# A delta-rule stage's closing LayerNorm and the next one, done per group inside its output loop

## The chip, the cores and the metric

One core of one Trainium2 chip runs the whole program. The metric is the device time in microseconds of one execution. Three runs of the kernel before took 3671.51, 3671.94 and 3673.90 us; the median is 3671.94.

## The reference

Four layers, each a mixer and a feed-forward part behind a LayerNorm, with residuals, on x of 4 x 1024 x 128 (fp32). What matters here is the end of the fourth mixer and the LayerNorm behind it:

```python
        out = SCALE * out / (denominator + EPS)
        layer_out = jnp.transpose(out, (2, 0, 1, 3)).reshape(slen, bsz, N_HEAD * D_HEAD)
        attn_out = jnp.einsum('sbi,oi->sbo', layer_out, W_o)
        x = h + attn_out
        mu = x.mean(-1, keepdims=True)
        var = ((x - mu) ** 2).mean(-1, keepdims=True)
        return (x - mu) / jnp.sqrt(var + LN_EPS) * ln_g + ln_b
...
    x = x + _L3_attn_ref(_layernorm(x, axis=-1), L3_attn_W_qkvb, L3_attn_W_o, L3_attn_ln_g, L3_attn_ln_b)
    x = x + _L3_ffn_ref(_layernorm(x, axis=-1), L3_ffn_gate_w, L3_ffn_experts)
```

Here h is the normalised input of the mixer, and ln_g, ln_b are vectors of 128 channels. The delta rule runs over the 4 batch entries (the reference calls the first axis the sequence), so for each of the 1024 positions and 16 heads the output of entry t is a sum over the values of entries 0 to t, with scalar weights alpha.

## The kernel before

X holds the residual stream and XN the normalised one, each 128 partitions x 32 tiles x 128 channels (tile t * 8 + j is positions 128 j to 128 j + 127 of batch entry t). XT holds the normalised stream transposed, 128 channels x 4096 tokens. `delta_rule` (from L2164) is a row of stages; each `Stage` ends with a barrier of all engines. The stage "alg" computes alpha on VectorE. The stage "out" works in 8 groups j of 4 units t; n = 4 j + t counts the units, and every engine follows its own list, in order, tied to the others by semaphores:

- TensorE: `sums(j, t)` (L2628) transposes the accumulated heads of unit n, 8 times 128x128, when VectorE has them (`acc_ready`). `values(j + 1, t)` (L2620) makes the values of the same t one group ahead, two matmuls of 512 columns. `project(n - 1)` (L2639) multiplies the transposed heads of the unit before with W_o, 8 matmuls of 128 columns into one of two banks `po`. Each fp32 matmul stands as two records in the profile, a transpose as one.
- ScalarE: two copies of the transposes of unit n out of PSUM into `lT` (L2671), then `take` (L2660), two copies of the values one group ahead.
- VectorE: for unit n one product into `acc` (L2694), t products (L2699) and t additions (L2707), all 128x1024, so 1, 3, 5 and 7 instructions for t = 0 to 3. It may write `acc` of unit n when unit n - 2 is transposed. Behind them `finish(n - 2)` (L2685) waits for the projection of unit n - 2 (`out_mm`) and adds it to the normalised input in XN.

Behind the stage "out" three stages follow. `layernorm` (from L131) on XN, without transposes: 32 BATCH_NORM_STATS2 (L151), a few small instructions, a root on ScalarE (L190), a reciprocal (L164), 32 normalisations (L167), all on VectorE but the root. The stage "fin" loads gain and offset to all partitions, and three VectorE instructions over 128x4096 (L2728 to L2730) scale XN, add the offset to X, and add the two. Then `program` (from L2939) calls `layernorm` on X before the last feed-forward part, this time with 32 transposes on TensorE (L185) and 8 copies on ScalarE (L201) into XT. The next stage, "sink" (`sinkhorn_gates`), begins with a small DMA (L2768) and 32 matmuls that read all of XT (L2780).

Of the kernel before, what the change touches and what calls it, by code (L numbers as in the profile page):

```python
# [15 lines left out]
ALU = mybir.AluOpType  # L16
# [3 lines left out]
P = 128  # L20
BATCH, SEQ, C = 4, 1024, 128
T = BATCH * SEQ
NT = T // P
# [107 lines left out]
def layernorm(nc, X, XN, XT, ident, name, affine=None):  # L131


    with Stage(nc, name) as s:
        stats = s.sb("stats", [P, NT, 6])
        mean, var, tmp, rstd = (s.sb(n, [P, NT]) for n in ("mean", "var", "tmp", "rstd"))
        eps = s.sb("eps", [P, 1])
        aff = s.sb("aff", [P, 2])
        aff_in = s.sem("aff_in")
        tp = [s.ps(f"tp{k}") for k in range(2)]  # L140
        stats_done, var_ready, std_ready, rstd_ready, xn_ready, t_ready, t_copied = (s.sem(n) for n in (
            "stats_done", "var_ready", "std_ready", "rstd_ready", "xn_ready", "t_ready", "t_copied"))
        ch = s.sem("vector_chain")
        with nc.Block() as block:

            @block.vector
            def _(dve):
                c = Chain(dve, ch)
                nc.vector.memset(eps[:], LN_EPS).then_inc(stats_done, 1)
                for i in range(NT):  # L150
                    nc.vector.bn_stats(stats[:, i], X[:, i]).then_inc(stats_done, 1)  # L151
                dve.wait_ge(stats_done, NT + 1)

                nc.vector.tensor_tensor(mean[:], stats[:, :, 1], stats[:, :, 4], ALU.add).then_inc(ch, 1)
                nc.vector.tensor_tensor(tmp[:], stats[:, :, 1], stats[:, :, 4], ALU.subtract).then_inc(ch, 1)
                nc.vector.tensor_tensor(var[:], stats[:, :, 2], stats[:, :, 5], ALU.add).then_inc(ch, 1)
                dve.wait_ge(ch, 3)
                c.n = 3
                c.link(nc.vector.tensor_scalar(mean[:], mean[:], 0.5, None, ALU.mult))
                c.link(nc.vector.tensor_tensor(tmp[:], tmp[:], tmp[:], ALU.mult))  # L160
                c.link(nc.vector.tensor_scalar(tmp[:], tmp[:], 0.25, None, ALU.mult))
                nc.vector.scalar_tensor_tensor(var[:], var[:], 1.0 / C, tmp[:], ALU.mult, ALU.add).then_inc(var_ready, 1)
                dve.wait_ge(std_ready, 1)
                nc.vector.reciprocal(rstd[:], tmp[:]).then_inc(rstd_ready, 1)  # L164
                dve.wait_ge(rstd_ready, 1)
                for i in range(NT):
                    nc.vector.tensor_scalar(XN[:, i], X[:, i], mean[:, i:i + 1], rstd[:, i:i + 1],  # L167
                                            ALU.subtract, ALU.mult).then_inc(xn_ready, 1)

                dve.wait_ge(xn_ready, NT)  # L170

            @block.sync
            def _(sp):
                if affine:
                    for k in range(2):
                        sp.dma_start(aff[:, k:k + 1], affine[k].rearrange("(c a) -> c a", a=1)).then_inc(aff_in, 16)

            @block.tensor
            def _(pe):
                for i in range(NT if XT is not None else 0):  # L180
                    g, k = divmod(i, TPG)
                    pe.wait_ge(xn_ready, i + 1)
                    if k == 0 and g >= 2:
                        pe.wait_ge(t_copied, g - 1)
# [3 lines left out]
            def _(act):  # L188
                act.wait_ge(var_ready, 1)
                nc.scalar.activation(tmp[:], var[:], ACT.Sqrt, bias=eps[:]).then_inc(std_ready, 1)  # L190
                if XT is None:
                    return
# [2802 lines left out]
```

## Time and profile before

| | us |
|---|---|
| median of three runs | 3671.94 |
| profiled execution | 3670.11 |
| its span | 3668.4 |
| output loop (3193.6 to 3404.3) | 210.7 |
| three stages behind it (to 3460.8) | 56.5 |
| the rest of the program behind them | 207.6 |

Over the span TensorE's matmuls are busy 73%, VectorE 58%, ScalarE 39%, GpSimd 26%, and TensorE's mean granted clock is 0.845 of full speed. Such shares are means over many stages with other limits; for a change in one stage its own stretch has to be read, in order of time: what each engine does, how long it stood before it, and which engine released it.

### The profile page before, as it was taken

How to read it: one execution, taken by the hardware profiler on the slowest of the kernel's cores; microseconds unless marked ns; L12 is line 12 of the kernel's file. 1: busy time of each engine (PE TensorE's matmuls, PEld its weight loads, DVE VectorE, ACT ScalarE, POOL GpSimd, SP SyncE). 2: the span in 40 equal slices, each digit the busy share in tenths (PEclk: the TensorE clock that was granted, in tenths of full speed). 3: DMA queues.
4: the chain of work that ended last, by engine and by line, in shares of the span. 5: the costliest groups of instructions: out<-in, count | busy, mean ns of one | idle time of the engine just before them, and what ended most of it. 6: DMA issues, size and time to landing. Idle time of an engine off the chain costs nothing. (4 is left out here: it accounts for less than half of the span.)

```text
span 3668.4 us, 31380 instructions
## 1 busy us (share of the span) xinstructions
PE 2677.9 (73%) x8896; PEld 1455.9 (40%) x8904; DVE 2129.6 (58%) x3695; ACT 1420.2 (39%) x3926; POOL 951.0 (26%) x620
## 2 busy tenths in 40 slices
PE   2007888999999889999877766782687787377317
PEld 1003344555555544444344442351344443255303
DVE  7997531222222366565534458013999996678686
ACT  1004333111111156666543320231798898233003
POOL 0003565000000000000122210303899999000005
PEclk6558999999999989999878879896887787689557
DMA  2001112000000074545200020112000000000001
GB/s 51 0 0 47 47 48 62 0 0 0 0 0 0 13 148 139 147 138 143 74 1 1 1 72 1 50 46 69 1 1 1 1 1 1 23 1 1 2 0 29
DMA packets 106429, 124.40 MB, mean 34 GB/s; under 512 B 21771, under 2 KB 59788, under 8 KB 106028
## 3 DMA queue, kind: packets, MB, share of 16 engines
q1 hardware_dynamic: 104236, 118.56, 12.2%
q0 software_dynamic: 2048, 4.20, 0.4%
q8 instruction: 55, 0.90, 0.1%
q14 instruction: 90, 0.74, 0.1%
HBM read 108.55 MB, written 14.16 MB: 33 GB/s over the span
## 5 line engine op out<-in xcount | busy, mean ns | idle before, releaser
L2325 POOL TENSOR_TENSOR dots_pr<-dots_g 128x1536 f32<-128x1536 f32 (+3 forms) x118 | 356.5, 3063 | 66.6 <-DVE dots_g L2450 54.0
L1012 DVE SCALAR_TENSOR_TENSOR attn_sim<-attn_sc,attn_mask 128x512 f32<-128x512 f32 (+3 forms) x256 | 125.8, 491 | 316.9 <-PE attn_sc L938 313.8
L938 PE MATMUL attn_sc<-attn_q,attn_xb 128*128 128x512 f32 (+3 forms) x768 | 295.0, 486 | 0.0
L949 PE MATMUL attn_op<-attn_sim,attn_v 128*128 128x512 f32 (+3 forms) x768 | 295.0, 486 | 0.0
L1298 DVE TENSOR_TENSOR grp_h<-grp_sq,grp_cb 128x512 f32<-128x512 f32 x256 | 176.5, 692 | 191.9 <-ACT grp_sq L1186 171.8
L1126 PE MATMUL grp_po<-grp_h,grp_down 128*128 128x512 f32 x512 | 266.4, 602 | 5.7 <-DVE grp_h L1298 5.7
L1118 PE MATMUL grp_ph<-all_xt,grp_up 128*128 128x512 f32 x512 | 264.0, 598 | 0.5 <-ACT grp_sg L1202 0.5
L2338 PE MATMUL dots_pu<-delta_wE,all_xt 128*128 128x264 f32 x512 | 193.3, 524 | 97.0 <-DVE dots_g L2450 95.6
L1180 ACT ACTIVATE grp_r<-grp_ph 128x512 f32<-128x512 f32 x272 | 162.4, 597 | 185.6 <-PE grp_ph L1118 183.9
L626 POOL TENSOR_TENSOR mix_h<-mix_r,mix_cb 128x512 f32<-128x512 f32 x128 | 179.4, 1413 | 123.8 <-ACT mix_r L540 90.3
L2392 ACT ACTIVATE dots_pr<-dots_pr 128x128 f32<-128x128 f32 x704 | 206.2, 300 | 3.5 <-POOL dots_pr L2325 3.5
L938 PEld LDWEIGHTS attn_sc<-attn_q,attn_xb 128*128 128x128 f32 x768 | 141.0, 190 | 125.7 <-issue 107.1
L2338 PEld LDWEIGHTS dots_pu<-delta_wE,all_xt 128*128 128x128 f32 x512 | 118.6, 249 | 175.8 <-DVE dots_g L2450 148.9
L2325 POOL TENSOR_TENSOR all_xn<-dots_g 128x1536 f32<-128x1536 f32 (+3 forms) x58 | 180.1, 3137 | 3.3 <-PE dots_fold L2348 3.3
L949 PEld LDWEIGHTS attn_op<-attn_sim,attn_v 128*128 128x128 f32 x768 | 141.0, 190 | 98.4 <-issue 68.9
L2447 DVE TENSOR_TENSOR dots_m<-dots_pu,dots_sg 128x512 f32<-128x512 f32 x256 | 164.7, 685 | 24.7 <-ACT dots_sg L2373 14.4
L2348 PE MATMUL dots_fold<-dots_pr,all_ident 128*128 128x512 f32 x336 | 160.0, 632 | 25.3 <-ACT dots_pr L2379 25.3
L378 PE MATMUL mix_po<-mix_woT,mix_y 128*128 128x128 f32 x128 | 17.1, 298 | 213.7 <-DVE mix_y L738 213.7
L2450 DVE SCALAR_TENSOR_TENSOR dots_g<-dots_m,dots_pu 128x512 f32<-128x512 f32 x256 | 163.3, 679 | 0.0
L1186 ACT ACTIVATE grp_sq<-grp_r 128x512 f32<-128x512 f32 x256 | 159.1, 621 | 0.0
L987 ACT ACTIVATE attn_sim<-attn_sc 128x512 f32<-128x512 f32 x128 | 76.4, 597 | 205.6 <-PE attn_sc L938 205.6
L1126 PEld LDWEIGHTS grp_po<-grp_h,grp_down 128*128 128x128 f32 x512 | 94.4, 191 | 138.8 <-issue 95.9
(612 smaller groups left out, 5341.5 us busy)
## 6 DMA issues: line engine op xcount, KB each, us to landing
grp_cb<-grp_combine SPq DMA_DIRECT2D x512, 128.0 KB, 3.2
mix_cb<-top_weights SPq DMA_DIRECT2D x64, 256.0 KB, 3.2
cap_xs<-cap_zero SPq DMA_DIRECT2D x7, 320.0 KB, 4.6
experts_xe<-cap_xs SPq DMA_DIRECT2D x7, 320.0 KB, 3.3
all_x<-in_L_attn_x_dram SPq DMA_DIRECT2D x4, 512.0 KB, 5.4
cap_w<-in_L_ffn_W_dram SPq DMA_DIRECT2D x1, 2048.0 KB
cap_ys<-experts_yo SPq DMA_DIRECT2D x8, 256.0 KB, 2.3
delta_h<-all_xn SPq DMA_DIRECT2D x1, 2048.0 KB
```

Of the source, the lines that this page charges most:

```text
L626: nc.gpsimd.tensor_tensor(h[:, J % HB], r[:, J % RB], cb[:, n % CB], ALU.mult).then_inc(h_ready, 1)
L938: nc.tensor.matmul(sc[k % SC][:, 0:w], xb[:, m * P:(m + 1) * P], q[:, par, n0:n0 + w], start=True, stop=True).then_inc(s_mm, 1)
L949: ins = nc.tensor.matmul(op[half][:, n0 - half * GROUP:n0 - half * GROUP + w], v[:, par, m], sim[:, par, k, 0:w], start=False, stop=False)
L1118: nc.tensor.matmul(ph[J % 2][:], w, XT[:, g * GROUP:(g + 1) * GROUP], start=True, stop=True).then_inc(up_mm, 1)
L1126: nc.tensor.matmul(po[g % 2][:], w, h[:, J % HB], start=(j == 0), stop=(j == NJ - 1)).then_inc(down_mm, 1)
L1180: nc.scalar.activation(r[:, J % RB], ph[J % 2][:], ACT.Relu).then_inc(relu_done, 1)
L1298: tt(h[:, J % HB], sq[:, J % RB], cb[:, n % CB], ALU.mult).then_inc(h_done, 1)
L2325: nc.gpsimd.tensor_tensor(dst, a, key, ALU.mult).then_inc(pp_ready, 1)
L2338: ins = nc.tensor.matmul(heads(n % PB)[:, q * HQ:(q + 1) * HQ], XTj[:, k // 2, j], wE[:, 1 - k % 2, h0:h0 + HQ], start=True, stop=True)
L2392: ins = nc.scalar.activation(v_, v_, ACT.Relu, accum_out=dots[:, 8 + r, j, h0:h0 + 1])
L2447: tt(m[:, sh], x[..., sh + 1:sh + 1 + D_], sg[:, n % PB], ALU.mult).then_inc(m_ready, 1)
L2450: ins = stt(g[:, I % 2, k, :, sh * D_:(sh + 1) * D_], m[:, sh], 0.0, x[..., 0:D_], ALU.max, ALU.mult)
```

## The change

The stage "out" also does what the three stages behind it did; those are removed, as are `layernorm` and its call in `program`. In the loop:

- `project` adds the normalised input by a matmul of the identity with XN's tile into the same bank, so `po` holds the new sum. There is one bank `po` instead of two, and unit n waits for `x_done` of unit n - 1; the other bank is `tr`.
- `finish` moves from VectorE to ScalarE: a copy of `po` into XN whose accumulator gives the sum over channels (`total`). On ScalarE it is `finish(n - 1)`, behind the copies of unit n.
- When the four units of a group are finished, the group goes through six steps, each in a unit of the loop, counted from n = 4 j: STATS at + 4 (ScalarE: mean, four Squares with a pointer bias and an accumulator, root), NORM at + 5 (VectorE: reciprocal and product; ScalarE: four Identities with pointer scale and bias), TURN at + 6 (TensorE: four transposes; ScalarE: one copy into `xnT`), GAIN at + 7 (TensorE: for each of four tiles a matmul with a diagonal matrix of the gain, one of a row of ones with the offset, one of the identity with X; ScalarE: four copies with accumulator into X, and the second statistics), NORM_2 at + 8, TURN_2 at + 9 (four transposes, one copy into XT).
- On VectorE `factors(n)` stands behind the sums of unit n: for NORM (t = 1) and NORM_2 (t = 0) it waits for the root of that group (`std_ready`).
- The loop runs on behind its last unit until the last group has gone through all steps. Two small DMAs at the start load gain and offset.

```diff
-            po = [s1.ps(f"po{k}") for k in range(2)]
+            po, tr = s1.ps("po"), s1.ps("tr")
+            NN = JT * S
+            LAST = NN + 7
+            STATS, NORM, TURN, GAIN, NORM_2, TURN_2 = 4, 5, 6, 7, 8, 9
+            def due(n, at):
+                j, k = divmod(n - at, S)
+                return j if k == 0 and 0 <= j < JT else None
...
                     def project(n):
...
                         pe.wait_ge(lT_ready, n + 1)
-                        if n >= 2:
-                            pe.wait_ge(x_done, n - 1)
+                        if n:
+                            pe.wait_ge(x_done, n)
                         for a in range(HD // P):
-                            ins = nc.tensor.matmul(po[n % 2][:, 0:C], lT[:, n % 2, a], woT[:, a], start=(a == 0), stop=(a == HD // P - 1))
-                        ins.then_inc(out_mm, 1)
+                            nc.tensor.matmul(po[:, 0:C], lT[:, n % 2, a], woT[:, a], start=(a == 0), stop=False)
+                        nc.tensor.matmul(po[:, 0:C], ident[:], XN[:, t * JT + j], start=False, stop=True).then_inc(out_mm, 1)
+                    def late(n):
...
+                        j = due(n, GAIN)
+                        if j is not None:
+                            pe.wait_ge(xnT_ready, j + 1)
+                            for t in range(S):
+                                y = tr[:, t * P:(t + 1) * P]
+                                nc.tensor.matmul(y, xnT[:, t * P:(t + 1) * P], diag[:], start=True, stop=False)
+                                nc.tensor.matmul(y, ones_row[:], shift_row[:], start=False, stop=False)
+                                ins = nc.tensor.matmul(y, ident[:], X[:, t * JT + j], start=False, stop=True)
+                            ins.then_inc(y_mm, 1)
...
                 def _(act):
+                    def finish(n):
...
+                        act.wait_ge(out_mm, n + 1)
+                        if j and t == 0:
+                            act.wait_ge(factors_ready, 2 * j - 1)
+                        nc.scalar.activation(XN[:, t * JT + j], po[:, 0:C], ACT.Copy, accum_out=total[:, 0, t:t + 1]).then_inc(x_done, 1)
+                    def statistics(j, second, src):
+                        c.link(nc.scalar.activation(negm[:, second], total[:, second], ACT.Copy, scale=-1.0 / C))
+                        for t in range(S):
+                            ins = nc.scalar.activation(square[:, t], src[:, t * JT + j], ACT.Square, bias=negm[:, second, t:t + 1],
+                                                       accum_out=spread[:, second, t:t + 1])
+                        c.link(ins)
+                        nc.scalar.activation(dev[:, second], spread[:, second], ACT.Sqrt, bias=eps[:], scale=1.0 / C).then_inc(std_ready, 1)
+                    def normalise(j, second, src):
+                        act.wait_ge(factors_ready, 2 * j + 1 + second)
+                        for t in range(S):
+                            ins = nc.scalar.activation(XN[:, t * JT + j], src[:, t * JT + j], ACT.Identity,
+                                                       bias=move[:, second, t:t + 1], scale=rstd[:, second, t:t + 1])
+                        ins.then_inc(normed, 1)
...
                             take(j + 1, t)
+                            finish(n - 1)
+                            late(n)
+                    for n in range(NN, LAST + S):
+                        finish(n - 1)
+                        late(n)
...
                 def _(dve):
+                    def factors(n):
+                        for second, at in enumerate((NORM, NORM_2)):
+                            j = due(n, at)
+                            if j is not None:
+                                dve.wait_ge(std_ready, 2 * j + 1 + second)
+                                c.link(nc.vector.reciprocal(rstd[:, second], dev[:, second]))
+                                tt(move[:, second], negm[:, second], rstd[:, second], ALU.mult).then_inc(factors_ready, 1)
...
-                            finish(j * S + t - 2)
+                            factors(n)
```

## Rows read from the trace of the kernel before

**Rows 1.** Busy time by stretch: loop, then the stages behind; engines, clock, DMA.
```profile
...
3193.60:3404.30 210.70, 163.31 (x896) 123.43 (x896) 156.23 (x160) 70.69 (x128) 0.00 (x0) 0.89 0.00 1
3404.30:3460.80 56.50, 8.28 (x32) 5.44 (x32) 45.56 (x150) 6.70 (x11) 0.00 (x1) 0.57 0.01 3
...
```

**Rows 2.** Timeline of one period of the output loop: start, length, engine, line, idle before.
```profile
...
3269.68 1.22 DVE L2694 TENSOR_TENSOR out_acc<-out_v,delta_alpha 128x1024 f32<-128x1024 f32 x1
3269.71 1.94 PE L2628 MATMUL out_pt<-all_ident,out_acc 128*128 128x128 f32 x8 [3.83 <-DVE out_acc L2707]
...
3271.44 2.47 PE L2620 MATMUL out_pv<-delta_wv,all_xt 128*128 128x512 f32 x4
...
3273.75 1.95 PE L2639 MATMUL out_po<-delta_woT,out_lT 128*128 128x128 f32 x16
...
3275.80 0.29 DVE L2685 TENSOR_TENSOR all_xn<-out_po,all_xn 128x128 f32<-128x128 f32 x1 [4.91 <-PE out_po L2639]
3276.01 1.22 DVE L2694 TENSOR_TENSOR out_acc<-out_v,delta_alpha 128x1024 f32<-128x1024 f32 x1
...
3280.32 1.22 DVE L2694 TENSOR_TENSOR out_acc<-out_v,delta_alpha 128x1024 f32<-128x1024 f32 x1
...
3286.31 1.22 DVE L2694 TENSOR_TENSOR out_acc<-out_v,delta_alpha 128x1024 f32<-128x1024 f32 x1
3286.34 1.06 PE L2628 MATMUL out_pt<-all_ident,out_acc 128*128 128x128 f32 x8 [1.89 <-DVE out_acc L2707]
...
3287.24 1.88 PE L2620 MATMUL out_pv<-delta_wv,all_xt 128*128 128x512 f32 x4
3287.44 1.08 ACT L2671 ACTIVATE out_lT<-out_pt 128x512 f32<-128x512 f32 x2 [4.15 <-PE out_pt L2628]
...
3288.41 1.35 ACT L2660 ACTIVATE out_v<-out_pv 128x512 f32<-128x512 f32 x2
...
3294.71 1.22 DVE L2694 TENSOR_TENSOR out_acc<-out_v,delta_alpha 128x1024 f32<-128x1024 f32 x1
...
3296.47 3.60 PE L2620 MATMUL out_pv<-delta_wv,all_xt 128*128 128x512 f32 x4
...
```

**Rows 3.** Timeline of ScalarE, an earlier stage: ACTIVATE with accumulator, then its read.
```profile
...
3105.72 0.29 ACT L2392 ACTIVATE dots_pr<-dots_pr 128x128 f32<-128x128 f32 x1
3105.92 0.19 ACT L2392 ACTIVATION_READ_ACCUMULATOR dots_pr<-dots_pr 128x1 f32 x1
3106.01 0.29 ACT L2392 ACTIVATE dots_pr<-dots_pr 128x128 f32<-128x128 f32 x1
...
```

**Rows 4.** Groups by line and form, ScalarE: busy, mean ns of one, idle before.
```profile
...
L2907 ACT ACTIVATE exp_part<-exp_po,exp_coef 128x128 f32<-128x128 f32 x128 | 34.7, 382 | 115.6 <-PE exp_po L2895 115.6
...
L516 ACT ACTIVATE all_xt<-mix_tr,mix_aff 128x512 f32<-128x512 f32 x8 | 6.2, 777 | 9.0 <-PE mix_tr L387 9.0
...
L512 ACT ACTIVATE mix_dev<-mix_var,mix_eps 128x8 f32<-128x8 f32 x4 | 1.2, 300 | 0.0
...
```

**Rows 5.** Timeline, end of the output loop's first group on VectorE.
```profile
...
3218.52 1.22 DVE L2694 TENSOR_TENSOR out_acc<-out_v,delta_alpha 128x1024 f32<-128x1024 f32 x1
...
```

**Rows 6.** Timeline of the loop's end and of the stages behind it.
```profile
...
3388.23 1.53 PE L2628 MATMUL out_pt<-all_ident,out_acc 128*128 128x128 f32 x8 [3.15 <-DVE out_acc L2707]
...
3396.62 1.94 PE L2628 MATMUL out_pt<-all_ident,out_acc 128*128 128x128 f32 x8 [3.91 <-DVE out_acc L2707]
...
3398.36 5.63 PE L2639 MATMUL out_po<-delta_woT,out_lT 128*128 128x128 f32 x32
...
3413.80 0.35 DVE L164 RECIPROCAL ln_rstd<-ln_tmp 128x32 f32<-128x32 f32 x1 [0.39 <-ACT ln_tmp L190]
...
3460.79 0.33 SPq L2768 DMA_DIRECT2D sink_gw<-in_L_ffn_gate_w_dram  x1
...
```

**Rows 7.** Groups by line and form, ScalarE: a table load, and the Squares.
```profile
...
L1186 ACT ACTIVATE grp_sq<-grp_r 128x512 f32<-128x512 f32 x256 | 159.1, 621 | 0.0
...
L1202 ACT ACT_TABLE_LOAD x1 | 1.3, 1283 | 0.0
...
```

More of the change, by code:

```diff
@@ L128, in wait_turned @@
         eng.wait_ge(self.xt_ready, groups)
[L131 to L184, printed above, removed]
-                    nc.tensor.transpose(tp[g % 2][:, k * P:(k + 1) * P], XN[:, i], ident[:]).then_inc(t_ready, 1)
-            @block.scalar
[L188 to L192, printed above, removed]
-                if affine:
-                    act.wait_ge(aff_in, 32)
-                for g in range(NG):
-                    act.wait_ge(t_ready, TPG * (g + 1))
-                    dst = XT[:, g * GROUP:(g + 1) * GROUP]
-                    if affine:
-                        ins = nc.scalar.activation(dst, tp[g % 2][:], ACT.Identity, bias=aff[:, 1:2], scale=aff[:, 0:1])
-                    else:
-                        ins = nc.scalar.activation(dst, tp[g % 2][:], ACT.Copy)
-                    ins.then_inc(t_copied, 1)
-                act.wait_ge(t_copied, NG)
@@ new lines, in late @@
+                    def late(n):
+                        j = due(n, TURN)
+                        if j is not None:
+                            pe.wait_ge(normed, 2 * j + 1)
+                            pe.wait_ge(xt_ready, j)
+                            turn(j)
+                        j = due(n, GAIN)
[7 more added lines that the diff above has]
+                            ins.then_inc(y_mm, 1)
+                        j = due(n, TURN_2)
+                        if j is not None:
+                            pe.wait_ge(normed, 2 * j + 2)
+                            pe.wait_ge(y_taken, j + 1)
+                            turn(j)
@@ L2648, in _ @@
                             project(j * S + t - 1)
-                    project(JT * S - 1)
+                            late(j * S + t)
+                    for n in range(NN, LAST + S):
+                        project(n - 1)
+                        late(n)
                 @block.scalar
@@ L2673, in _ @@
                             take(j + 1, t)
+                            finish(n - 1)
+                            late(n)
+                    for n in range(NN, LAST + S):
+                        finish(n - 1)
+                        late(n)
+                    act.wait_ge(xt_ready, JT)
+                @block.sync
+                def _(sp):
+                    sp.dma_start(gain[:], ln_g.rearrange("(c a) -> c a", a=1)).then_inc(affine_in, 16)
+                    sp.dma_start(shift_row[:], ln_b.rearrange("(a c) -> a c", a=1)).then_inc(affine_in, 16)
+                @block.gpsimd
+                def _(pool):
+                    nc.gpsimd.memset(eps[:], LN_EPS).then_inc(consts, 1)
+                    nc.gpsimd.memset(ones_row[:], 1.0).then_inc(consts, 1)
                 @block.vector
@@ L2708, in _ @@
                                 ins.then_inc(added if r < t else acc_ready, 1)
[L2709 to L2730 removed]
+                            factors(n)
+                    for n in range(NN, LAST + S):
+                        factors(n)
 def sinkhorn_gates(nc, XT, ident, gate_w, coef):
```

84 lines of the change are left out of this document (54 added, 30 removed).

## The prediction

> **What bounds the kernel now.** I read the busy times by stage first, then one period of the output loop in order of time, then the stretch behind the loop. The output loop runs from 3193.6 to 3404.3 us, 210.7 us, with VectorE busy for 156 of them and TensorE for 163 [rows 1]. It has 8 groups j of 4 units, n = 4j + t. A period is 25.03 us (VectorE starts t = 0 at 3269.68 and again at 3294.71 [rows 2]); VectorE's own work in it is 19.1: 1.2 for t = 0, then 3.7, 5.9 and 8.3 (the starts 3276.01, 3280.32, 3286.31, 3294.71 less the finish and its wait). Most of the rest is one wait: at t = 0 `finish` needs the projection of t = 2, which TensorE can only do behind the transposes of t = 3; VectorE stands for 4.91 us [rows 2]. Behind the loop come 56.5 us in which little else than VectorE works (45.6 us busy): LayerNorm, scale and offset, LayerNorm with transposes [rows 1]. Nothing hides them.
>
> **What is removed.** All of those 56.5 us, and `finish` from VectorE: its 4.91 us wait and 4 x 0.2 us per group. Were nothing added in their place, VectorE would take 19.1 us a group and TensorE some 22 (per unit transposes 0.87, values 1.71, projection 1.8 by the starts in [rows 2], 0.22 for the identity matmul, then 16 records of turning, 24 of gain): the loop would shrink too.
>
> **What is added on VectorE: two waits in its queue.** `factors(n)` stands right behind the sums of unit n and waits for a root that ScalarE takes in unit n - 1, in all but the first group. VectorE runs ahead of TensorE and ScalarE by about one unit, so both waits are real. What is queued behind them is the sums of t = 1 (behind NORM_2 at t = 0) and of t = 2 (behind NORM at t = 1), and everybody waits for those. I follow the chain, with 0 at the end of the sums of t = 3:
>
> 1. TensorE, unit t = 3. In unit t = 2 of before it is 4.7 us from the end of the sums (3286.2) to the end of the projection: transposes 1.06, values 1.88, projection 1.95, overlapping [rows 2]. Behind it now lie the identity matmul (2 records) and 12 gain matmuls (24 records), at 1.79/16 = 0.11 each: 0.22 + 2.67. The gain is ready at 7.6.
> 2. ScalarE: four copies with accumulator. The trace has this pair: start to start 0.29 us, the 0.19 us read of the accumulator lies beside the next ACTIVATE [rows 3]. So 3 x 0.29 + 0.39 = 1.3. Then the mean (0.2, below the 0.30 of a root over 128x8), four squares (3 x 0.29 + 0.38 + 0.1 = 1.4) and the root (0.30) [rows 4], with some 0.03 for each wait on itself: 3.3 together. Root at 10.9.
> 3. VectorE: a reciprocal and a product of 128x4. The reciprocal of 128x32 takes 0.35 [rows 6]; two short ones cannot be under 0.12 or over 0.7; I take 0.4. Then t = 1, 3.65: done at 14.95.
> 4. Meanwhile ScalarE does unit t = 0, 4 copies of 512 columns at 0.5 (two in 1.08 [rows 2]), finish 0.4 and the first statistics 2.0: 4.4 behind the root, at 15.3. VectorE waits 0.35 more, 0.4 for the factors: 15.75.
> 5. t = 2 and t = 3: 5.9 + 8.3. The end is at **30.0** us, with TensorE at full clock, against 25.0 before.
>
> TensorE and ScalarE (about 19 us a group) are not the bound; the sum of hand-overs is.
>
> **The clock.** Before t = 3 TensorE idles 3.8 us and then starts at the lower of its two levels, 1.2 GHz: 8 transposes take 1.94 instead of 1.06 and the values 2.47, once 3.60, instead of 1.88, which puts the projection's end 1.4 to 2.6 us later [rows 2]. After 1.89 us of idling it stays at 2.4 GHz [rows 2]; after 3.15 it is between, 1.53 for the same transposes [rows 6]. In the new period TensorE ends unit t = 2 (sums at 21.7, then 4.7 + 0.2 + 0.45 for the turn) at about 26.9 and idles 3.2 us before t = 3. That is nearest to the 3.15 row. All that is lost there is on the chain: bounds 0 and 2.6, taken 1.5. Period **31.5**.
>
> **The loop.** VectorE's t = 3 of the first group ended at 3218.4 [rows 5]; two finishes less put it at 3218.2. The second group has only the first statistics: 6.1 us to the end of the projection of t = 2 (cold, as at 3269.6 to 3275.7 [rows 2]), 4.6 for unit t = 0 with its projection, finish 0.4, statistics 2.0 and one table load 1.28 [rows 7], factors 0.4, then 5.9 + 8.3, with 0.3 for identity matmuls and hand-overs: 29.2. Six groups of 31.5 follow, 0.3 less in the last, which takes no values. The sums end at 3218.2 + 29.2 + 189.0 - 0.3 = 3436.1; before they ended at 3396.5 [rows 6]. The loads of gain and offset land while VectorE would wait for the first values anyway; cost nothing, 2 us at most if they are late.
>
> **The drain.** From the end of the last sums, TensorE cold as before (transposes 1.94, then 32 records in 5.63, 0.18 each [rows 6]): transposes, projection and gain of group 6 ready at 8.6; copies and second statistics 12.0; finish and first statistics of group 7 at 14.4; normalisations of group 6 and then 7 at 15.8 and 17.0; turn and copy of group 6 at 17.6, turn and copy of group 7 at 19.2; gain at the low clock (24 x 0.21) 24.3; copies and statistics 27.7; factors 28.1; normalise 29.6; turn and copy 31.2; stage end 0.9: 32.1 us. A normalising Identity with two pointers lies between 0.27 (34.7/128, one pointer) and 0.48; I took 0.3 to 0.35 [rows 4]. Before, the same way from 3396.5 to the next stage's first DMA at 3460.8 was 64.3 [rows 6]. So 32.2 are won here.
>
> The Trainium skill, ScalarE: Activation LUTs, in the paragraph on what the ACTIVATE instruction costs, has a price for this: each pointer operand adds about 93 ns. By it the four Identities of a normalisation would be spaced 0.39 and take 1.6 instead of 1.4, three times on the drain's path: the sum 0.7 us longer. The one-pointer row's 382 ns agrees with it, its spacing of 0.27 is less; no row here shows the spacing with two.
>
> **Sum.** 3436.1 + 32.1 = 3468.2 against 3460.8: +7.4 us. The next stage is the same and starts with the clock down either way. The profiled execution took 3670.1 us (span 3668.4 and 1.7 around it), 1.8 below the median of 3671.94; the difference goes on the median: **3679.3 us**. The break-even period is (181.4)/6 = 30.2 us, so every microsecond of the period is six in the result.
>
> **Rivals.**
>
> - *The clock stays up* (not slower). One mechanism: at t = 3 of groups 2 to 7 the 3.2 us of idling do not lower the clock. It decides between 1.89 us (never lowered) and 3.8 (always) [rows 2]. Period 30.0, result 9 us less: 3670.5, no difference. For it speaks that the stretch of work before is dense; against it the 3.15 row.
> - *ScalarE's accumulator costs its whole 0.19* where the source is PSUM or the function a Square with a pointer: 13 pairs on the chain of each group, 2.5 us, and 20 in the drain: some 20 us more, 3699. Against it stands [rows 3], though that is SBUF and Relu.
> - *A table load before every Square and every root.* 4 x 1.28 us on each group's chain, 6 groups, and three statistics of the drain: 31 + 8 us more, 3718. In the trace 256 Squares follow one load for a Sigmoid without a load of their own [rows 7], so Square is at home in that set; whether it is in the root's no row shows.
> - *The waits are covered* (faster): if VectorE came late enough to each root that it found it done, the loop would run at TensorE's 22 us or so and the loads between, about 24.6 a group: 34 us less than before, 3638. It would need VectorE's sums to be behind ScalarE; the orders written out forbid it, as the chain above shows. I keep it for an error of mine in the orders.
>
> The Trainium skill speaks for the third: ScalarE: Activation LUTs, in its section on table sets ("the hidden batching unit"), asks to batch activations by set, and lists copy, relu, identity and abs as in every set, not square. By it the time would be the 3718. No stretch of this trace has a Square next to a Sqrt.
>
> **How the numbers follow.** Forecast (period 31 to 33) 0.50, clock up 0.27, dear accumulator 0.10, table loads 0.05, covered waits 0.08. A measurement of this kernel can tell 0.2%, 7.3 us, from no change; the forecast lies just at that edge, so its half is split 0.33 slower, 0.16 same and 0.01 faster. Slower 0.33 + 0.15, and 0.01 of the clock case if its drain is longer: 0.49; same 0.16 + 0.25 = 0.41; faster 0.10. The range leaves out the table loads and the covered waits: from the clock case less 2 us for short factors and 2 for a short drain, 3666.5, to the dear accumulator's 3699.
>
> **What would show it.** VectorE in the loop: idle before the reciprocals, about 9.5 us at t = 0 and 0.4 at t = 1, released by ScalarE's roots, 11 us a group; no wait for the projection. A period of 31.5 between its t = 0 starts. Transposes of t = 3 near 1.5 to 1.9 us. One table load in the stage. About 31 us between the last sums and the last copy into XT. The prediction is wrong if the roots are ready when VectorE asks, if more than one table load stands in the loop, or if ScalarE's pairs are spaced other than 0.29 us.

## The result and the profile after

The kernel after takes 3687.1 us (median of 6 runs, 3686.1 to 3689.1), the kernel before beside it 3671.7 (6 runs, 3667.5 to 3673.9): ratio 1.0041, 95% interval 1.0030 to 1.0052, so 15.4 us or 0.4% slower. The forecast was +7.4 us. The profiled execution of after took 3688.53 (span 3686.8) and that of before 3670.11; their difference, 18.4, is 3.0 more than that of the medians, since the one lies 1.4 above its median and the other 1.6 below.

First the busy times of two stretches of after: the loop up to 3438.00, shortly before its last sums end, and what follows, the drain (columns: stretch, TensorE, weight loads, VectorE, ScalarE and GpSimd with instructions, granted clock, DMA share, GB/s; the weight loads were not among the columns of [rows 1]'s reading).

```profile
...
3194.50:3438.00 243.50, 194.52 (x1112) 146.72 (x1112) 149.69 (x153) 140.40 (x430) 0.22 (x2) 0.92 0.00 1
3438.00:3478.00 40.00, 23.25 (x104) 18.87 (x104) 4.63 (x10) 16.37 (x67) 0.00 (x0) 0.66 0.00 1
...
```

The last sums end 45.2 us later than before (3441.68 against 3396.5 [rows 6]), and the next stage's first DMA comes 38.2 us behind them, where it came 64.3 behind: 26 us are won there, and 19 are missing in all. In the loop neither VectorE (149.7 of 243.5 us) nor ScalarE (140.4) is full; TensorE is busy for 194.5. The list of waits says who is late. VectorE, stage "out", columns: what waited, for whom, us in total, times, longest:

```profile
...
DVE out_rstd L2731 <- ACT out_dev L2654: 117.8, 15, 16.4
...
```

VectorE stands 117.8 us for roots of ScalarE, 15 times; 32.2 of them are the three waits in the drain (13.67, 2.13 and 16.39), the rest lies in the loop. The wait for the projection, the 4.91 us of [rows 2], is gone. The timeline of VectorE shows where the waits lie. The first and last rows are the t = 0 products, that is the start of a period (start, length, what, and in brackets the idle time before it):

```profile
...
3312.90 1.22 DVE L2743 TENSOR_TENSOR out_acc<-out_v,delta_alpha 128x1024 f32<-128x1024 f32 x1
3325.67 0.18 DVE L2731 RECIPROCAL out_rstd<-out_dev 128x4 f32<-128x4 f32 x1 [11.55 <-ACT out_dev L2654]
...
3330.06 0.18 DVE L2731 RECIPROCAL out_rstd<-out_dev 128x4 f32<-128x4 f32 x1 [0.40 <-ACT out_dev L2654]
...
3344.35 1.22 DVE L2743 TENSOR_TENSOR out_acc<-out_v,delta_alpha 128x1024 f32<-128x1024 f32 x1
3358.81 0.18 DVE L2731 RECIPROCAL out_rstd<-out_dev 128x4 f32<-128x4 f32 x1 [13.24 <-ACT out_dev L2654]
...
3377.49 1.22 DVE L2743 TENSOR_TENSOR out_acc<-out_v,delta_alpha 128x1024 f32<-128x1024 f32 x1
...
```

A period is 3344.35 - 3312.90 = 31.45 us, the next one 33.14. In both VectorE waits twice: 11.55 or 13.24 us behind t = 0, and 0.40 behind t = 1. The whole row of t = 0 starts is 3218.83, 3248.32, 3279.77, 3312.90, 3344.35, 3377.49, 3408.95, and the last sums end at 3441.68: 29.49 for the second group, then 31.45, 33.13, 31.45, 33.14, 31.46 and 32.73.

What VectorE waits for is the chain from its own sums of t = 3 back to the root. One period in order of time, TensorE and ScalarE:

```profile
...
3313.13 1.06 PE L2571 MATMUL out_pt<-all_ident,out_acc 128*128 128x128 f32 x8 [1.62 <-DVE out_acc L2756]
...
3317.76 0.39 PE L2602 MATMUL out_tr<-out_diag,out_xnT 128*128 128x128 f32 x2
...
3318.07 0.48 PE L2603 MATMUL out_tr<-out_shift_row,out_ones_row 1*128 1x128 f32 x2
...
3318.49 0.49 PE L2604 MATMUL out_tr<-all_x,all_ident 128*128 128x128 f32 x2
...
3318.81 0.39 PE L2602 MATMUL out_tr<-out_diag,out_xnT 128*128 128x128 f32 x2
...
3322.18 0.28 ACT L2679 ACTIVATE all_x<-out_tr 128x128 f32<-128x128 f32 x1 [3.85 <-PE out_tr L2604]
...
3325.27 0.30 ACT L2654 ACTIVATE out_dev<-out_spread,out_eps 128x4 f32<-128x4 f32 x1
...
```

Transposes at 3313.13; the gain's twelve matmuls from 3317.76 until 3321.98, where the next unit's transposes start, 4.2 us; ScalarE's copies from 3322.18, then the Squares; the root at 3325.27; the reciprocal of the timeline above at 3325.67.

### The profile page after: what moved, and what is told of

Its sections match the earlier page's. It is cut to its first block and busy times, and to the rows that moved or that the text cites. A ratio compares the mean times of both kernels' runs of the same rounds, so it can differ in the third digit from the quotient of the medians.

```text
span 3686.8 us, 32119 instructions
## 1 busy us (share of the span) xinstructions
PE 2725.6 (74%) x9192; PEld 1496.8 (41%) x9192; DVE 2081.2 (56%) x3547; ACT 1501.1 (41%) x4284; POOL 951.5 (26%) x622
```

## What the experiments had to tell apart

The theory of the forecast (A in the expectations): both waits for roots stand in the queue of VectorE, and what is queued behind them, the sums of t = 1 and t = 2, is what everybody else needs next. So one group is a ring of hand-overs VectorE, TensorE, ScalarE, VectorE, and every microsecond in it is six in the result. The rivals: the loop is long because there is more work on TensorE and ScalarE, wherever the waits stand; or because the steps are too early in the order, and would be free a unit or two later. Two prices inside the ring were disputed: the offset matmul with one row (C), and the low clock of TensorE (E). The experiments ran in three sets, each with runs of the kernel before in it (medians 3670.7, 3675.2 and 3678.1). So each kernel is given by its ratio to the before of its own set, with the 95% interval, and two kernels of different sets are compared by the distances of their medians from their own before (after: +15.4 us). An interval is some 4 us to either side; a difference of 4 us between two kernels is therefore weak by itself, and the timelines have to carry it.

### The steps one unit later

The first try at a cure by order: NORM, TURN, NORM_2 and TURN_2 one unit later, the guard on the old factors moved to `statistics`.

```diff
-            STATS, NORM, TURN, GAIN, NORM_2, TURN_2 = 4, 5, 6, 7, 8, 9
+            STATS, NORM, TURN, GAIN, NORM_2, TURN_2 = 4, 6, 7, 7, 9, 10
```

> The changed kernel with other due units: NORM at + 6, TURN and GAIN at + 7, NORM_2 at + 9, TURN_2 at + 10 (were 5, 6, 7, 8, 9), and the guard on the factors moved from finish to the statistics. Same instructions, same work, but VectorE comes to each root about a unit later. Theory A (VectorE stands in its own queue for the roots, 11.6 to 13.2 us and 0.4 us a group): the waits before the reciprocals fall under 1 us, the period becomes TensorE's, 4 x 4.6 + 0.9 for the turns + 4.2 for the gain + about 1 for the copy between turn and gain = 24.5, to 27 with a low clock at times; seven groups of 25.5 instead of 31.5 to 33 bring 3642 us (3630 to 3660). Theory B (the added work on ScalarE and TensorE sets the period, whoever waits): 3687 within 5.

Measured: 3670.8 us, 0.9994 of before [0.9985, 1.0004]. That is some 15 us less than after, a third of the 45 expected and outside the range; neither theory's number came. VectorE's timeline, one group:

```profile
...
3304.89 1.22 DVE L2743 TENSOR_TENSOR out_acc<-out_v,delta_alpha 128x1024 f32<-128x1024 f32 x1
...
3320.51 0.18 DVE L2731 RECIPROCAL out_rstd<-out_dev 128x4 f32<-128x4 f32 x1 [10.50 <-ACT out_dev L2654]
...
3326.61 0.17 DVE L2731 RECIPROCAL out_rstd<-out_dev 128x4 f32<-128x4 f32 x1
...
```

The first root is found ready (3326.61 has no idle time before it). The second one still costs 10.50 us here and 8.97 in the group before, now behind t = 1. A unit of delay in the order can be worth no more than what VectorE does in that unit, and t = 1 is short, 3.65 us; the second root also comes 1.3 us later in the period than in after (3290.30 - 3276.21 = 14.09 against 12.77). The period is 28.7 to 31.5 us.

### The factors on GpSimd

The wait is taken out of VectorE's queue and nothing else is moved: GpSimd, which has nothing to do in this stage, waits for the roots, raises them to the power -1 and takes the product.

```diff
+                    for n in range(LAST + S):
+                        for second, at in enumerate((NORM, NORM_2)):
...
+                                pool.wait_ge(std_ready, 2 * j + 1 + second)
+                                c.link(nc.gpsimd.tensor_tensor(rstd[:, second], dev[:, second], one[:], ALU.pow))
+                                nc.gpsimd.tensor_tensor(move[:, second], negm[:, second], rstd[:, second], ALU.mult).then_inc(factors_ready, 1)
...
-                            factors(n)
```

> The changed kernel with the same due units, but the reciprocal (as a power of -1) and the product of factors run on GpSimd, which is idle in this stage. Only VectorE's two waits for ScalarE's roots are gone; ScalarE's and TensorE's lists are the same. Theory A: period about 24 to 27, 3645 us (3630 to 3660); the two GpSimd operations cost up to 1 us each and are covered. Theory B (added work sets the period): 3687 within 5.

Measured: 3637.2 us, 0.9907 [0.9891, 0.9924]: 33 us less than before, some 49 less than after. VectorE:

```profile
...
3291.39 1.22 DVE L2745 TENSOR_TENSOR out_acc<-out_v,delta_alpha 128x1024 f32<-128x1024 f32 x1
...
3301.62 1.23 DVE L2745 TENSOR_TENSOR out_acc<-out_v,delta_alpha 128x1024 f32<-128x1024 f32 x1 [5.10 <-PE out_pt L2572]
...
3315.62 1.22 DVE L2745 TENSOR_TENSOR out_acc<-out_v,delta_alpha 128x1024 f32<-128x1024 f32 x1
...
```

A period is 3315.62 - 3291.39 = 24.23 us, and all periods from 3242.94 on are within 0.01 of it. GpSimd's power in the loop and in the drain:

```profile
...
3308.60 2.05 POOL L2730 TENSOR_TENSOR out_rstd<-out_dev,out_minus_one 128x4 f32<-128x4 f32 x1 [2.29 <-ACT out_dev L2655]
...
3420.24 1.01 POOL L2730 TENSOR_TENSOR out_rstd<-out_dev,out_minus_one 128x4 f32<-128x4 f32 x1 [15.47 <-ACT out_dev L2655]
...
```

TensorE and ScalarE do the same work in the same order as in after, and in the loop the factors take longer than on VectorE (1.8 to 2.1 us for the power and 0.25 for the product, against 0.18 and 0.16; up to 1 us each was expected). So it was not the amount of work on TensorE and ScalarE that made after slow, but whose queue the wait stands in. (The order is worth something too, 15 us in the version above, but it only moves the wait.) What is left on VectorE is 5.10 us before t = 2: TensorE transposes the sums of t = 0 only behind the gain of the group before.

### The offset with all rows

The offset's matmul takes 128 rows instead of one (127 of them zero in the offset, ones on the other side); the sum that it adds is the same.

```diff
-            gain, shift_row, ones_row, diag = s1.sb("gain", [P, 1]), s1.sb("shift_row", [1, C]), s1.sb("ones_row", [1, P]), s1.sb("diag", [P, C])
+            gain, shift_row, ones_row, diag = s1.sb("gain", [P, 1]), s1.sb("shift_row", [P, C]), s1.sb("ones_row", [P, P]), s1.sb("diag", [P, C])
...
-                    sp.dma_start(shift_row[:], ln_b.rearrange("(a c) -> a c", a=1)).then_inc(affine_in, 16)
+                    sp.wait_ge(zeroed, 1)
+                    sp.dma_start(shift_row[0:1], ln_b.rearrange("(a c) -> a c", a=1)).then_inc(affine_in, 16)
```

> The changed kernel, but the matmul that adds the offset has 128 rows (all ones by a matrix whose first row is the offset and the rest zero) instead of one row. Theory C (the one-row matmul keeps the next weights from being loaded ahead: 1.05 us for three matmuls instead of 0.66): the gain of four tiles falls from 4.2 to 2.7 us, it lies on VectorE's wait, so the period falls by 1.5 and the result by 7 x 1.5 + 2 = 12 us, to 3675 (3671 to 3679). Theory D (three matmuls into one place cost 1.05 whatever their rows): 3687 within 4.

Measured: 3672.7 us, 1.0006 [0.9997, 1.0016], some 13 us less than after. TensorE, the gain of the first tile and the start of the second:

```profile
...
3283.12 0.39 PE L2603 MATMUL out_tr<-out_diag,out_xnT 128*128 128x128 f32 x2
3283.35 0.39 PE L2604 MATMUL out_tr<-out_shift_row,out_ones_row 128*128 128x128 f32 x2
...
3283.79 0.39 PE L2603 MATMUL out_tr<-out_diag,out_xnT 128*128 128x128 f32 x2
...
```

A tile takes 0.67 us (3283.79 - 3283.12), three equal matmuls of 0.22; in after it takes 1.05 (3318.81 - 3317.76). There the one-row matmul begins 0.31 after the one ahead of it and its follower 0.42 after it. Four tiles give 1.5 us a group, and the shorter period falls by just that, to 29.92 (3278.27 to 3308.19) from 31.45. The longer one falls by 1.85, to 31.28 (3308.19 to 3339.47) from 33.13; 0.3 of that is not the tiles'. What in the one-row matmul costs the time (Theory C has the weight loads) is not shown by this; the time goes away with the form.

### Only the finish on ScalarE

From the kernel before: only the first part of the change, the identity matmul and `finish` as a copy on ScalarE, behind unit n + 1's copies. The three stages behind the loop stay.

```diff
-                        ins.then_inc(out_mm, 1)
+                        nc.tensor.matmul(po[n % 2][:, 0:C], ident[:], XN[:, t * JT + j], start=False, stop=True).then_inc(out_mm, 1)
...
+                            finish(n - 1)
...
-                            finish(j * S + t - 2)
```

> The kernel before with one part of the change alone: the normalised input is added by the identity matmul, finish is a copy on ScalarE, one unit later than its projection, two banks as before; the three stages behind the loop stay. Theory A (VectorE's 4.9 us wait for the projection and its four finishes set 25.0 us a period): the period falls to 19.1 + 0.7 to 1.8 for the transposes at t = 1, 20 to 21 us, and the result to 3636 us (3630 to 3645). Theory B (TensorE's own work and its low clock set the period): 3672 within 6.

Measured: 3638.9 us, 0.9909 [0.9892, 0.9925], 32 us less than before. VectorE:

```profile
...
3284.79 1.22 DVE L2697 TENSOR_TENSOR out_acc<-out_v,delta_alpha 128x1024 f32<-128x1024 f32 x1
...
3304.79 1.22 DVE L2697 TENSOR_TENSOR out_acc<-out_v,delta_alpha 128x1024 f32<-128x1024 f32 x1
...
```

A period is 20.00 us instead of 25.03, with 1.1 us of waits beside some 19 of work. So the change as made is a gain of 32 us and a loss of 47: the steps between the units cost 47 us more than the 56.5 us of stages that they replace [rows 1].

### Factors and offset on GpSimd

Both findings together. The factors as above; the offset is added to X by GpSimd ahead of the loop's gain (32 additions of 128x128), so the gain has two matmuls a tile.

```diff
-                                nc.tensor.matmul(y, ones_row[:], shift_row[:], start=False, stop=False)
...
+                            nc.gpsimd.tensor_tensor(xt, xt, shift_all[:], ALU.add).then_inc(x_plus, 1)
```

> As e2 (factors on GpSimd), and the offset is added to X by 32 additions on GpSimd at the start of the stage, so that the gain has two full matmuls a tile instead of three, one of them of one row. Theory A, with the cycle read from e2 (end of t = 3's sums, TensorE's whole unit with the gain, transposes of t = 0, sums of t = 2 and t = 3: 24.2 us): the gain falls from 4.2 to 8 x 0.22 = 1.8, the period to 21.8, seven of them 17 us and the drain 5 us shorter than e2's: 3615 us (3610 to 3622). Rival: ScalarE, with some 20 us of work a group, or GpSimd's additions beside VectorE hold the period at 24: 3632 to 3637.

Measured: 3619.5 us against 3675.2 of before in the same set, 0.9847 [0.9832, 0.9862]: 56 us less than before. This is the fastest version found. VectorE in the loop, and first one row of its first group:

```profile
...
3215.67 4.27 DVE L2753 TENSOR_TENSOR out_part<-out_v,delta_alpha 128x1024 f32<-128x1024 f32 x3
...
3290.40 1.22 DVE L2748 TENSOR_TENSOR out_acc<-out_v,delta_alpha 128x1024 f32<-128x1024 f32 x1
...
3298.18 1.23 DVE L2748 TENSOR_TENSOR out_acc<-out_v,delta_alpha 128x1024 f32<-128x1024 f32 x1 [2.67 <-PE out_pt L2573]
...
3312.19 1.22 DVE L2748 TENSOR_TENSOR out_acc<-out_v,delta_alpha 128x1024 f32<-128x1024 f32 x1
...
```

The period is 21.79, and the wait for the transposes is 2.67 instead of 5.10: the 2.43 us are the gain's, which has gone from 1.05 to 0.44 a tile. GpSimd's additions:

```profile
...
3200.41 35.91 POOL L2724 TENSOR_TENSOR all_x<-all_x,out_shift_all 128x128 f32<-128x128 f32 x32 [3.30 <-DMA out_shift_all<-in_L_attn_ln_b_dram]
...
```

They take 35.9 us, 1.12 each, while the loop's first groups run.

### TensorE kept at its clock

To price the low clock alone: ten matmuls of the identity with itself, into a bank that is free then and that nobody reads, behind unit t = 2 of every group but the first (18 in the last).

```diff
+                            if t == 2 and j:
+                                for _k in range(10 if j < JT - 1 else 18):
+                                    nc.tensor.matmul(pt[1][0][:, 0:P], ident[:], ident[:], start=True, stop=True)
```

> The changed kernel, with 10 identity matmuls of 128 columns (2.2 us) put on TensorE behind unit t = 2 of each group, 18 in the last, whose result nobody reads; they fill most of its 3 us of idling before t = 3. Theory E (the periods of 33.1 instead of 31.45 us, three of seven, and the slow start of the drain come from the lower clock after that idling): all periods 31.45, 3 x 1.7 + 3 us less, 3679 us (3676 to 3682). Rival (the longer periods have another cause, or so short a filling does not hold the clock): 3687 within 3, or more if the filling comes in the way.

Measured: 3685.0 us, 1.0028 [1.0017, 1.0038] against after's 1.0041 [1.0030, 1.0052], some 5 us less, with intervals that overlap; 3679 (3676 to 3682) was expected, and the rival's 3687 lies nearer. TensorE:

```profile
...
3310.09 2.40 PE L2626 MATMUL out_pt<-all_ident 128*128 128x128 f32 x20
3313.22 1.06 PE L2571 MATMUL out_pt<-all_ident,out_acc 128*128 128x128 f32 x8 [0.74 <-DVE out_acc L2759]
...
```

2.4 us of the gap are filled, 0.74 are left, and the transposes of t = 3 take 1.06. The t = 0 starts from 3281.55 on are 3312.99, 3344.43, 3375.88 and 3407.32: each period 31.44, where after has 33.1 in every other. The one long period left, 33.40 from 3248.15 on, is the filling's own doing: in the second group the unit ahead of it ran at the low clock, the ten matmuls came at 3248.14 and held the transposes of t = 3 until 3250.37. So the timelines show what the medians alone leave open: the alternation of after is the clock, and it costs 1.69 us a time. In the profiled executions, 6.1 us apart up to the next stage's first DMA (3473.74 against 3479.84), that is three times 1.69 less, 1.95 more in the one long period, and 2.8 less in the drain, which is 35.4 us instead of 38.2. The filling's own cost is the part that the expectation had left out.

### Only the second wait taken away

The second LayerNorm's factors on GpSimd, the first one's still on VectorE. By the list of waits that should take away nearly all of the 12 us a group.

```diff
+                    for j in range(JT):
+                        pool.wait_ge(std[1], j + 1)
+                        c.link(nc.gpsimd.tensor_tensor(rstd[:, 1], dev[:, 1], minus[:], ALU.pow))
+                        nc.gpsimd.tensor_tensor(move[:, 1], negm[:, 1], rstd[:, 1], ALU.mult).then_inc(fr[1], 1)
```

> The changed kernel with only the second LayerNorm's factors on GpSimd: VectorE's large wait (11.6 to 13.2 us at t = 0) is gone, the small one (0.4 us at t = 1, for the first statistics) stays in its queue. Theory A in its stronger form (the chain runs acc of t = 3, gain, second statistics, unit t = 0 with the first statistics on ScalarE; VectorE merely waits where it meets it): the wait reappears in full at t = 1, since the first root comes 17.2 us into the period as before; period 31.45 to 33.1, 3687 us within 3. Rival (each wait costs what the profile shows before it): 11.6 x 6 us less, down to e2's 3637.

Measured: 3686.7 us, 1.0033 [1.0022, 1.0043], some 4 us less than after, with intervals that overlap. VectorE:

```profile
...
3279.17 1.22 DVE L2752 TENSOR_TENSOR out_acc<-out_v,delta_alpha 128x1024 f32<-128x1024 f32 x1
3280.60 1.22 DVE L2752 TENSOR_TENSOR out_acc<-out_v,delta_alpha 128x1024 f32<-128x1024 f32 x1 [0.21 <-PE out_pt L2574]
...
3296.31 0.18 DVE L2740 RECIPROCAL out_rstd<-out_dev 128x4 f32<-128x4 f32 x1 [12.03 <-ACT out_dev L2657]
...
3310.61 1.22 DVE L2752 TENSOR_TENSOR out_acc<-out_v,delta_alpha 128x1024 f32<-128x1024 f32 x1
...
```

The wait behind t = 0 is gone; t = 1 starts 0.21 us behind it, at 3280.60. But behind t = 1 VectorE now waits 12.03 us instead of 0.40, for the first LayerNorm's root, and gets it 17.14 us into the period (3296.31 - 3279.17), where after has it at 17.16 (3330.06 - 3312.90). The period is 31.44 or 31.45 in every group from 3247.72 on; after's longer periods of 33.1, the low clock's, do not occur in this execution, which is nearly all that the loop gains. The 11.55 us wait that the list showed was worth nothing by itself.

### The steps two units later

The order once more, with NORM_2 and TURN_2 at + 10, their own semaphores, and NORM_2's factors ahead of NORM's.

```diff
-            STATS, NORM, TURN, GAIN, NORM_2, TURN_2 = 4, 5, 6, 7, 8, 9
+            STATS, NORM, TURN, GAIN, NORM_2, TURN_2 = 4, 6, 7, 7, 10, 10
...
-                        for second, at in enumerate((NORM, NORM_2)):
+                        for second, at in ((1, NORM_2), (0, NORM)):
```

> As e1, but NORM_2 and TURN_2 at + 10, so that VectorE asks for the second root behind the sums of t = 2 and no longer behind the short ones of t = 1; the lists of ScalarE and TensorE hold the same instructions. In e1 the chain was: transposes to gain of t = 3 with turn and copy in it 10.3 to 11.7 us, copies and second statistics 3.4, root at 14 to 15 us, while VectorE was there at 4.9: the waits of 9.0 to 10.5. Theory A: now VectorE is there at about 16 us, the second root is 2 us old, and it waits 2 to 3 us for the first root of the next group, at 18.4; then sums of t = 3, 8.2: period 27 (e1: 28.7 to 30.2), 3652 us (3645 to 3658). Rival (VectorE's queue is not what is left; ScalarE's or TensorE's own lists hold it at e1's level): 3671.

Measured: 3673.4 us against 3678.1 of before in its set, 0.9990 [0.9981, 1.0000], some 20 us less than after. 3652 (3645 to 3658) was expected; the rival, that TensorE's or ScalarE's own list holds it at 3671, is what came. VectorE:

```profile
...
3297.86 0.18 DVE L2733 RECIPROCAL out_rstd<-out_dev 128x4 f32<-128x4 f32 x1 [0.76 <-ACT out_dev L2656]
...
3321.72 1.23 DVE L2745 TENSOR_TENSOR out_acc<-out_v,delta_alpha 128x1024 f32<-128x1024 f32 x1 [9.37 <-PE out_pt L2573]
...
```

The root waits have shrunk to 0.76 here and 1.35 at most, as meant. In their place VectorE waits 6.49 or 9.37 us at t = 2 for transposes. TensorE says why:

```profile
...
3305.73 0.69 PE L2590 MATMUL out_tr<-all_ident,all_xn 128*128 128x128 f32 x4 [1.99 <-ACT all_xn L2661]
3306.58 1.94 PE L2573 MATMUL out_pt<-all_ident,out_acc 128*128 128x128 f32 x8 [0.17 <-DVE out_acc L2758]
...
3316.52 0.79 PE L2605 MATMUL out_tr<-out_shift_row,out_ones_row 1*128 1x128 f32 x2
...
```

It waits 1.99 us for the normalised tiles and, behind its next transposes of them, 0.69 for ScalarE's copy (before 3313.99), starts the transposes of t = 3 at the low clock (1.94), and in the middle of the gain the records go from 0.48 to 0.79 us. From the first gain record to the next unit's transposes it is then 5.7 us (3313.99 to 3319.70) instead of the 4.3 of the group before. The periods alternate between 27.3 (3279.07 to 3306.35) and 31.1 (3306.35 to 3337.42). The expectation had the ring's first wait right and did not ask what was late next.

## Why the prediction was right and where it was off

**The direction, the mechanism and the range held**, the size did not: +15.4 us where +7.4 was forecast. The direction was a narrow bet, 0.49 for slower against 0.41 for the same. Of the three signs by which the prediction called itself wrong, one came: ScalarE's pairs are not spaced 0.29 us (step 2). The account in the profiled executions, up to the next stage's first DMA (3479.84 against 3460.79 [rows 6], +19.05): 7.4 forecast, 0.9 because the stage began that much later, -0.3 in the first group, +0.3 in the second, +4.7 in the six groups, +6.1 in the drain, 19.1 in all. The medians are 3.7 us nearer to each other than that: 3.0 is where the two profiled executions lie about their medians, 0.65 is the rest of the program behind.

**What is removed.** Right. The projection's wait and `finish` on VectorE are worth 5.0 us a group (the version with the finish alone); 5.7 were removed, and 1.1 of new waits for transposes came instead.

**The two waits on VectorE.** Right in place and nearly in size: 11.55 and 0.40 against some 9.5 and 0.4. By the steps, with 0 at the start of t = 0:

1. Gain ready at 9.3 instead of 7.6 (3322.18 - 3312.90). This is the step that was off, a term of the sum mis-sized. The term "24 records at 0.11" was taken from full matmuls; with one-row matmuls between them 24 records take 4.2 us, not 2.67. The row that was missing is one with a single-row matmul; the trace of before had none, and the term had no bound above.
2. Root taken at 12.77 instead of 10.9: 1.7 of it is step 1's. That the 3.5 us between are so near the 3.3 forecast is luck, since two errors cancel: copies with accumulator are spaced 0.25, not 0.29, and Squares 0.39, not 0.29.
3. The factors 0.29 instead of 0.4.
4. The first root at 17.16 instead of 15.3, step 1's delay passed on.
5. The rest 14.0 instead of 14.2. End at 31.45 instead of 30.0, TensorE at full clock in both.

That after's shorter period, 31.45, is the forecast's 31.5 is luck: the forecast reached it by 30.0 and 1.5 for a low clock, and the chip by a longer gain at a clock that stayed up.

**The clock.** The mechanism was right, the term's form was not: 1.5 us in each of the groups was taken, and it is 1.69 in every other. TensorE's granted clock is 0.85 of full speed in the period from 3279.77, 1.00 in the next, then 0.90 and 1.00. Transposes of t = 3 and the values behind them, in after:

```profile
...
3280.00 1.60 PE L2571 MATMUL out_pt<-all_ident,out_acc 128*128 128x128 f32 x8 [2.97 <-DVE out_acc L2756]
...
3344.58 1.35 PE L2571 MATMUL out_pt<-all_ident,out_acc 128*128 128x128 f32 x8 [2.97 <-DVE out_acc L2756]
3345.73 3.33 PE L2563 MATMUL out_pv<-delta_wv,all_xt 128*128 128x512 f32 x4
...
3377.72 1.06 PE L2571 MATMUL out_pt<-all_ident,out_acc 128*128 128x128 f32 x8 [2.97 <-DVE out_acc L2756]
...
3409.18 1.10 PE L2571 MATMUL out_pt<-all_ident,out_acc 128*128 128x128 f32 x8 [2.97 <-DVE out_acc L2756]
3410.08 3.58 PE L2563 MATMUL out_pv<-delta_wv,all_xt 128*128 128x512 f32 x4
...
```

The idle time before t = 3 is 2.97 us in these four groups (forecast 3.2). In three of them the clock falls, each time while the work behind the gap already runs: transposes of 1.60, 1.35 and 1.10 us, with values of 3.07, 3.33 and 3.58 behind them, 4.7 us for the two together each time. In the fourth it stays up: 1.06 and 1.88. So idle time alone does not decide it here. The other two groups in which it stays up had less of it: 1.62 us before 3313.13, under 0.1 before the transposes at 3248.54. With three of the six groups warm the periods cost 193.4 us together, 4.7 more than the 188.7 forecast: 1.45 x 6 = 8.7 more from the steps, 4.0 less from the clock (three times 1.69 instead of six times 1.5, and smaller differences).

**The drain.** Forecast 32.1, measured 38.2 (3441.68 to 3479.84); before it was 64.3 [rows 6]. Rows of it:

```profile
...
3451.93 0.28 ACT L2679 ACTIVATE all_x<-out_tr 128x128 f32<-128x128 f32 x1 [3.92 <-PE out_tr L2604]
...
3463.30 0.80 PE L2602 MATMUL out_tr<-out_diag,out_xnT 128*128 128x128 f32 x2 [0.69 <-ACT out_xnT L2674]
...
3464.02 0.79 PE L2603 MATMUL out_tr<-out_shift_row,out_ones_row 1*128 1x128 f32 x2
...
3471.19 0.28 ACT L2679 ACTIVATE all_x<-out_tr 128x128 f32<-128x128 f32 x1 [7.95 <-PE out_tr L2604]
...
3479.84 0.34 SPq L2798 DMA_DIRECT2D sink_gw<-in_L_ffn_gate_w_dram  x1
...
```

Group 6's gain is ready at 10.3 instead of 8.6; group 7's, at the low clock, takes 7.9 us (3463.30 to 3471.19) instead of 5.1, since at that clock a one-row matmul takes 0.72 to the start of its follower, the matmul ahead of it 0.56 to 0.72 and the one behind it 0.59 (in the version with all rows the first of the twelve takes 0.59 and each other 0.43, 5.3 us in all); and the end of the stage takes 1.4 (3478.48 to 3479.84) instead of 0.9. That is 5.0 of the 6.1; the rest was not followed up. The last copy into XT ends 36.8 us behind the last sums, where about 31 was given as a sign.

**The price of the one row.** The version with all rows shows that the offset's form costs 13 us in the result. Priced right, the forecast would have been some 20 us above before instead of 7, and so 5 too high by the medians, 1.5 by the profiled executions. So the miss of 8 us is smaller than its one large error: the clock's term, 4 us too dear, hid a part of it, and up to 3.7 are no term of the sum, but lie between the executions and behind the stage.

**The rivals.** *The clock stays up* is true for three groups of six, but for only one of the four that had the idle time it speaks of. *ScalarE's accumulator costs its whole 0.19* and *a table load before every Square* are both answered by the groups of lines (columns: busy us, mean ns of one, idle before):

```profile
...
L2659 ACT ACTIVATE all_xn<-all_xn,out_move,out_rstd 128x128 f32<-128x128 f32 x32 | 13.1, 485 | 0.0
...
L2651 ACT ACTIVATE out_square<-all_xn,out_negm 128x128 f32<-128x128 f32 x32 | 12.5, 390 | 0.3
...
L2679 ACT ACTIVATE all_x<-out_tr 128x128 f32<-128x128 f32 x32 | 8.4, 278 | 35.0 <-PE out_tr L2604 35.0
...
L2654 ACT ACT_TABLE_LOAD x1 | 1.3, 1283 | 0.0
...
```

One table load stands in the whole stage, 1.3 us. Square, Sqrt, Copy and Identity alternate without another. What the Trainium skill, ScalarE: Activation LUTs, says in its section on table sets, that switching sets costs a load, with Square not in its list of functions that every set has, would by the prediction's reading have given 3718. The trace does not bear that reading out for Square with Sqrt. The accumulator's read is hidden but for about 0.1 us.

The price in the same page of the Trainium skill, in its paragraph on what the ACTIVATE instruction costs, about 93 ns for each pointer operand, agrees roughly: 278 ns without a pointer (from PSUM), 390 with one, 485 with two, so 112 and 95 ns, and the four Identities take 1.63 us together, the 1.6 that the rule gave. The prediction applied that rule to the Identities alone. The Squares have a pointer too, and their 0.39 is 0.29 and the same 0.1.

*The waits are covered*, the faster rival, did not come in after. That its number (3638) is what the kernel with the factors on GpSimd took (3637) goes with the period, 24.6 there and 24.23 here, reached by another way. It needed the wait out of VectorE's queue, not a slower VectorE.

## What to carry to other kernels

A wait for another engine's result should not stand in the queue of the engine that sets the pace, even where it is for two instructions of 0.2 us: here it closed a ring of three engines, and a reciprocal ten times slower on an engine that had nothing else to do made the kernel 49 us faster. The length of a wait in the profile is not its price; ask which release sets the time of the work behind it, and what is late next once it is gone (the second wait took over all of the first, and two later orders each met another). And where a stage that nothing hides is folded into a loop, price it against the loop without the fold: the parts here were worth 32 us less and 47 more.

## What was not expected of the hardware

- An fp32 matmul of a single row, 1x128 by 1x128, costs TensorE more than one of 128 rows: 0.42 us to the start of its follower instead of 0.22 at the high clock, 0.72 instead of 0.43 at the low one. In the trace its weight load and its follower's start together with the matmul, where the others start 0.11 us ahead of theirs; that this is the cause was not shown.
- With the same 2.97 us of idling before them the same eight transposes and the values behind them ran at full clock once and met a fall of the clock three times. At t = 1 it is the same with 3.06 us: 1.06 at 3329.80, 1.94 at 3298.35. Why was not settled; filling the gap to 0.74 us ended it.
- While GpSimd added 128x128 tiles in SBUF, VectorE's products of 128x1024 took up to 1.47 us instead of 1.22, and the same three products 4.27 instead of 3.49 us: the row at 3215.67 above, with GpSimd's 35.9 us run beside it. The first group of that kernel is 2.6 us longer than in the kernel with the factors alone on GpSimd (3201.47 to 3224.04 against 3201.29 to 3221.24). The Trainium skill, GPSIMD Engine Reference, in its section on specifications, says that its SBUF interfaces are shared with VectorE, with contention for instructions with two SBUF inputs; the products have two, and the row agrees. No version with another form of the products was tried.
- Four elements a partition raised to a power on GpSimd took 1.8 to 2.1 us in the loop but for the first, and 1.01 in the drain, where VectorE has no sums. Whether VectorE's work is the reason was not tested: the first ones of the two kernels, also in the loop, took 1.38 and 1.06.
